# A routing table made one stage later, and the order of scatters around a stage boundary

## The reference

```python
h = _layernorm(x, axis=-1) * (1 + ca) + sa
x = x + ga * _L0_attn_ref(h, ...)            # projections, a scan over time, a GELU network
h = _layernorm(x, axis=-1) * (1 + cb) + sb
x = x + gb * _L0_ffn_ref(h, ...)

# _L0_ffn_ref
gate_scores = softmax(einsum('btd,ed->bte', x, Wg))
topk_val, topk_idx = top_k(gate_scores, 2)   # shares, normalised to sum 1
for e in range(8):
    a, b = split(x @ W1[e].T + b1[e])
    out += ((a * sigmoid(b)) @ Wo.T + bo) * comb[..., e:e + 1]
```

## Time and profile before

| what | value |
|---|---|
| median of 3 runs | 766.77 us (761.83 to 767.51) |
| the profiled execution | 773.54 us, its span 771.7 us |
| busy: PE, PE weight load, DVE | 661.6, 517.8, 628.0 us |
| busy: ACT, POOL | 476.1, 534.8 us |
| mean granted clock of TensorE | 0.926 of full speed |
| DMA | 93.50 MB in 104898 packets |

### The profile page before, as it was taken

One profiled execution on the slowest core, in us unless ns is written; L12 is line 12 of the kernel. 1 busy time (PEld: TensorE's weight loads), 2 busy tenths in 40 slices (PEclk: granted clock), 3 DMA queues, 4 the chain that ended last, 5 costly groups with the idle time before them and its releaser, 6 DMA issues. The chain is left out here.

```text
span 771.7 us, 14151 instructions
## 1 busy us (share of the span) xinstructions
PE 661.6 (86%) x3705; PEld 517.8 (67%) x3705; DVE 628.0 (81%) x1408; ACT 476.1 (62%) x1167; POOL 534.8 (69%) x623
## 2 busy tenths in 40 slices
PE   2666799999999798988888978248999999999995
PEld 0443577777777566776666767036888888888884
DVE  5399999999999999989999467734777777777774
ACT  3665778999998696877656667212444444444442
POOL 4476767988888777899778754763655655655656
PEclk8798999999999999999999888566999999999998
DMA  4998888999898777878887486752444334434420
GB/s 118 253 135 131 100 129 136 132 131 157 147 139 152 95 126 123 138 169 157 139 149 138 125 254 180 201 153 64 80 68 81 71 62 71 74 64 78 77 49 2
DMA packets 104898, 93.50 MB, mean 121 GB/s; under 512 B 16251, under 2 KB 84438, under 8 KB 104694
## 3 DMA queue, kind: packets, MB, share of 16 engines
q1 hardware_dynamic: 87446, 77.62, 55.4%
q0 software_dynamic: 16176, 12.75, 9.5%
q10 hardware_dynamic: 1200, 2.23, 0.9%
HBM read 34.03 MB, written 25.61 MB: 77 GB/s over the span
## 5 line engine op out<-in xcount | busy, mean ns | idle before, releaser
L1870 POOL DMA_INDIRECT out<-res,index x91 | 141.3, 1553 | 103.2 <-DVE res L1938 86.4
L773 POOL TENSOR_TENSOR rs_prod<-rT,state_rows 128x512 f32<-128x512 f32 x128 | 139.1, 1094 | 45.6 <-DVE state_rows L1395 43.8
L1390 DVE TENSOR_TENSOR kv<-key,v_spread 128x512 f32<-128x512 f32 x128 | 84.6, 670 | 7.9 <-DMA v_spread<-vT 6.4
L1843 ACT ACTIVATE sig<-ps_a 128x256 f32<-128x256 f32 x91 | 35.1, 386 | 87.1 <-PE ps_a L1782 66.0
L1395 DVE TENSOR_TENSOR_SCAN state_rows<-decay,state_rows,kv 128x512 f32<-128x512 f32 x64 | 79.9, 1269 | 0.2
L1395 DVE TENSOR_TENSOR_SCAN state_rows<-decay,kv 128x512 f32<-128x512 f32 x64 | 76.1, 1209 | 0.2
L1907 DVE SCALAR_TENSOR_TENSOR half<-ps_b,xg,sig 128x256 f32<-128x256 f32 x91 | 44.0, 484 | 39.1 <-ACT sig L1845 34.4
L1177 PEld LDWEIGHTS ps_k<-w,gel 128*128 128x128 f32 x512 | 61.5, 200 | 13.4 <-issue 11.1
L1845 ACT ACTIVATE sig<-ps_b 128x256 f32<-128x256 f32 x91 | 35.0, 385 | 54.9 <-PE ps_b L1782 48.2
L1900 DVE SCALAR_TENSOR_TENSOR ps_a<-ps_a,xg,sig 128x256 f32<-128x256 f32 x91 | 44.4, 487 | 27.8 <-ACT sig L1843 19.7
L1177 PE MATMUL ps_k<-w,gel 128*128 128x128 f32 x512 | 64.3, 286 | 1.2 <-ACT gel L1015 1.2
(11 more groups left out here) (316 smaller groups left out, 2016.4 us busy)
## 6 DMA issues: line engine op xcount, KB each, us to landing
v_spread<-vT SPq DMA_DIRECT2D x128, 256.0 KB, 5.2
xg<-sorted_scratch SPq DMA_DIRECT2D x91, 130.0 KB
xin<-in_L_attn_x SPq DMA_DIRECT2D x16, 256.0 KB, 6.5
x<-in_L_attn_x SPq DMA_DIRECT2D x16, 256.0 KB, 5.2
out<-x SPq DMA_DIRECT2D x16, 256.0 KB
sorted_scratch<-gel SPq DMA_DIRECT2D x4, 910.0 KB, 8.2
tokens_scratch<-h SPq DMA_DIRECT2D x12, 256.0 KB
stage<-tokens_scratch SPq DMA_DIRECT2D x16, 128.0 KB, 4.8
```

Of the source, the lines that this page charges most:

```text
L773: pool.tensor_tensor(rs_prod[:, p, idx % 4], rT[p][:], state[idx][:, p * NT:(p + 1) * NT], ALU.mult).then_inc(s["rs_ready"], 1)
L1390: dve.tensor_tensor(kv[idx % 2][:], key[:], v_spread[idx % SPREADS][:], ALU.mult).then_inc(s["kv_ready"], 1)
L1870: pool.indirect_dma_start(out_rows, bass.IndirectOffsetOnAxis(ap=index[k % RESULTS][:, i:i + 1], axis=0), res[k % RESULTS][:, i, :], None, ...
```

## The change

- The early table is made with the counts after twelve of batch 2's sixteen groups (`IN_FRONT` = 12), so it gives 16 groups instead of 20. Only these twelve groups are scattered in the first stage; batch 2's other four join batch 3's sixteen in `list_late`, and the second stage's waits count 12 and 20.
- The early table's two columns are turned by PE in the turn of the last logits (`turn_table`) and copied by DVE at the start of the next turn (`keep_table`).
- The late table's twenty steps are made by DVE in the second stage, ten after pair 0's joins and ten after pair 1's; PE turns them into free parts of `ps_y` in front of the projections of pairs 2 and 3, and DVE copies them in pairs 3 and 4. SP and PE wait for `tables_set` at group 16, DVE for `left_set` at the first late pair.
- Batch 1's pair 6 is listed at spot 15, ahead of the layer norm operations of the last tile, instead of at spot 18; pair 7 stays at spot 19.
- On SP the `h3` stores of tiles 13 to 15 move from their place to the end of the turn.

The core of the diff:

```diff
+IN_FRONT = 12
-        self.end = off[:, :, off.shape[2] - 1:off.shape[2]].rearrange("p e g -> p (e g)")
+        self.end = off[:, :, end:end + 1].rearrange("p e g -> p (e g)")
...
-    early_groups = (EARLY * NT - (CLASSES - 1) * P) // P // 2 * 2
+    early_groups = (EARLY * NQ - (RG - IN_FRONT) - (CLASSES - 1)) // 2 * 2
...
                 for t, p, b in tile(8):
-                    after(sp, s["h3_ready"], t)
-                    if not isinstance(t, int) or t < early:
-                        sp.dma_start(pay_tiles[t], h3[p][:]).then_inc(s["h3_stored"][p], 16)
-                    else:
...
+                    if not isinstance(t, int) or t < VECTOR_ROWS:
+                        store_rows(t, p)
...
                 for t, p, b in tile(2):
                     spread_value(0, t, p)
                     spread_value(1, t, p)
+                for t, p, b in tile(8):
+                    if isinstance(t, int) and t >= VECTOR_ROWS:
+                        store_rows(t, p)
...
-                if r == LISTED - 2 and spot % 2 == 1 and spot < RG - 2:
+                if r == LISTED - 2 and spot % 2 == 1 and spot <= RG - 1:
                     list_pair(r, spot // 2 - 1)
-                if r == LISTED - 2 and spot >= RG + 2:
-                    list_pair(r, spot - RG // 2 - 4)
+                if r == LISTED - 2 and spot == RG + 3:
+                    list_pair(r, RG // 2 - 1)
...
-                    for m in range(RG // 2):
+                    for m in range(IN_FRONT // 2):
                         list_pair(r, m)
...
+                    beside(t, LAST, turn_table)
...
+            def turn_table():
+
+                pe.wait_ge(s["small_ready"], 1)
+                pe.wait_ge(s["table_step"], Table.EARLY_STEPS)
+                for c in range(2):
+                    mm = pe.transpose(ps_k1[0:1, c * P:(c + 1) * P], at[:, c:c + 1], ident[:])
+                mm.then_inc(s["table_ps"], 1)
...
-            run_pipeline(step, {WEIGHTS_AT: prepare_weights, BIAS_AT: split_bias, TABLE_AT: early_table})
-            late_table()
-            dve.wait_ge(s["table_ps"], 1)
...
+            run_pipeline(step, {WEIGHTS_AT: prepare_weights, BIAS_AT: split_bias, TABLE_AT: early_table, TABLE_AT + 1: keep_table})
...
                 if j == early_groups:
 
-                    sp.wait_ge(s["listed"], 16 * RG)
+                    sp.wait_ge(s["tables_set"], 1)
+                    sp.wait_ge(s["listed"], 16 * (2 * RG - IN_FRONT))
...
+                if k == TABLE_AT:
+                    pe.wait_ge(s["table_step"], Table.LATE_STEPS)
+                    for i, c in enumerate((4, 3)):
+                        pe.transpose(ps_y[0:1, (2 + i) * P:(3 + i) * P], at[:, c:c + 1], ident[:])
+                if k == TABLE_AT + 1:
+                    pe.matmul(ps_y[:, 2 * P:3 * P], at[:, 5:6].broadcast_to([P, P]), ident[:], start=True, stop=True)
...
-                for n in range(RG):
-                    g = LATE_BATCH + n
+                for n in range(IN_FRONT, 2 * RG):
+                    g = LAST_BATCHES + n
...
+                if k == 0:
+                    table.late_sizes()
+                    table.late_gaps()
+                    table.before()
+                    table.weigh_pairs()
+                    table.pairs()
+                if k == 1:
+                    table.weigh_rows()
+                    table.rows()
+                    table.late_place()
+                    table.class_ends()
+                    table.step_back()
+                if k == TABLE_AT + 1:
+                    keep_table()
+                if k == TABLE_AT + 2:
+                    leave_out()
```

More of the change, by code:

```diff
@@ L188, with __init__ @@
     EARLY_STEPS, LATE_STEPS = 14, 20
-    def __init__(self, dve, stepped, count, off, starts, pair_steps, ones, column, column1, work, done, at, stride):
+    def __init__(self, dve, stepped, count, off, starts, pair_steps, ones, column, column1, work, done, at, stride, end):
         self.dve, self.stepped, self.count = dve, stepped, count
@@ L369, in attention_block @@
      work, done, at, hits, mask, sel, pos, tot, off, carry_on, small, share, rs_prod, bias_all, v_spread, early_groups, late_groups, early) = kept
-    left_out = work[:].rearrange("p a e -> p (a e)")[:, 0:late_groups]
     NH2 = out_w.shape[1]
@@ L662, in step, with store_rows @@
                     spread_value(1, t, p)
+                for t, p, b in tile(8):
+                    if isinstance(t, int) and t >= VECTOR_ROWS:
+                        store_rows(t, p)
+            def store_rows(t, p):
+                after(sp, s["h3_ready"], t)
+                if not isinstance(t, int) or t < early:
+                    sp.dma_start(pay_tiles[t], h3[p][:]).then_inc(s["h3_stored"][p], 16)
+                else:
+                    sp.wait_ge(s["rs_ready"], TILES * DK)
+                    sp.dma_start(last_rows[:, (t - early) * NQ + RG:(t - early + 1) * NQ + RG, 0:P], h3[p][:]).then_inc(s["h3_stored"][p], 16)
             def stage_pair(r, m):
@@ L1305, in _ @@
             run_pipeline(step, {FIRST_PRODUCT_AT: await_weights, GATE_AT: await_gate})
-            pe.wait_ge(s["logits_ready"], TILES)
-            pe.wait_ge(s["table_step"], Table.EARLY_STEPS + Table.LATE_STEPS)
-            for i, c in enumerate((0, 1, 4, 3)):
-                pe.transpose(ps_m[0:1, i * P:(i + 1) * P], at[:, c:c + 1], ident[:])
-            pe.matmul(ps_k1[:, 0:P], at[:, 5:6].broadcast_to([P, P]), ident[:], start=True, stop=True).then_inc(s["table_ps"], 1)
         @block.vector
@@ L1619, in early_table @@
                 dve.wait_ge(s["route_step"], LISTED * Router.STEPS)
-                table = Table(dve, s["table_step"], 0, off[:], starts[:], pair_steps[:], ones[:, 0:CLASSES], column[:, 0:1], column[:, 1:2], work[:], done[:], at[:, 0:2], STRIDE)
+                table = Table(dve, s["table_step"], 0, off[:], starts[:], pair_steps[:], ones[:, 0:CLASSES], column[:, 0:1], column[:, 1:2], work[:], done[:], at[:, 0:2], STRIDE, IN_FRONT)
                 table.early_sizes()
@@ L1628, in early_table, with keep_table @@
                 table.place()
-            def late_table():
-                dve.wait_ge(s["route_step"], BATCHES * Router.STEPS)
-                table = Table(dve, s["table_step"], Table.EARLY_STEPS, off[:], starts[:], pair_steps[:], ones[:, 0:CLASSES], column[:, 0:1], column[:, 1:2], work[:], done[:], at[:, 2:6], STRIDE)
-                table.late_sizes()
-                table.late_gaps()
-                table.before()
-                table.weigh_pairs()
-                table.pairs()
-                table.weigh_rows()
-                table.rows()
-                table.late_place()
-                table.class_ends()
-                table.step_back()
+            def keep_table():
+                dve.wait_ge(s["table_ps"], 1)
+                dve.tensor_copy(row_table[:, 0:early_groups], ps_k1[0:1, 0:early_groups])
+                dve.tensor_scalar(pair_table[:, 0:early_groups], ps_k1[0:1, P:P + early_groups], float(H2 * PACK), None, ALU.add)
             def add_last(t, p, b):
@@ L1698, in expert_block @@
     PAIRS, EARLY_PAIRS = (GROUPS + 1) // 2, early_groups // 2
-    LOADS, RESULTS = 6, 4
-    LATE_BATCH = early * NQ
+    LOADS, RESULTS, TABLE_AT = 6, 4, 2
+    LAST_BATCHES = early * NQ - RG
     with ExitStack() as ctx:
@@ L1751, in load_group @@
                 if j == 0:
[L1752 removed]
+                    sp.wait_ge(rows_listed, 16 * IN_FRONT)
                 sp.dma_start(xg[:, slot(j), :], sorted_dram[bass.ds(row, P), :]).then_inc(s["x_in"][k % LOADS], 16)
@@ L1935, in finish @@
                     late = 2 * k - early_groups
+                    if late == 0:
+                        dve.wait_ge(s["left_set"], 1)
                     dve.tensor_tensor(index[k % RESULTS][:, 0:n], number, left_out[:, late:late + n], ALU.add)
@@ L1942, in _, with keep_table, leave_out @@
             dve.tensor_copy(parts[:], parts_f[:]).then_inc(s["parts_set"], 1)
+            def keep_table():
+                dve.wait_ge(s["y_ps"], TABLE_AT + 1)
+                dve.tensor_copy(row_table[:, early_groups:], ps_y[0:1, 2 * P:2 * P + late_groups])
+                dve.tensor_scalar(pair_table[:, early_groups:], ps_y[0:1, 3 * P:3 * P + late_groups], float(H2 * PACK), None, ALU.add).then_inc(s["tables_set"], 1)
+            def leave_out():
+                dve.wait_ge(s["y_ps"], TABLE_AT + 2)
+                dve.tensor_scalar(left_out, ps_y[:, 2 * P:2 * P + late_groups], column[:, 0:1], float(TILES * NT), ALU.is_gt, ALU.mult).then_inc(s["left_set"], 1)
+            table = Table(dve, s["table_step"], 0, off[:], starts[:], pair_steps[:], ones[:, 0:CLASSES], column[:, 0:1], column[:, 1:2], work[:], done[:], at[:, 2:6], STRIDE, RG)
             for n in range(E // 2):
```

13 lines of the change are left out of this document (4 added, 9 removed).

## The result

| | before | after |
|---|---|---|
| median of 13 runs each, one chip | 765.8 us (761.8 to 767.5) | 761.1 us (758.9 to 763.5) |
| the profiled execution | 773.5 us | 761.1 us |
| ratio of the times | | 0.9947, 95% interval 0.9930 to 0.9964 |

The changed kernel is 4.7 us faster there, half a per cent. The number forecast was 761.3.

The account below looks back on a forecast made before the run. PE sets the expert stage's pace, 5.28 us a pair; at the seam all engines wait for the last. Terms -6.5 + 0.6 + 0.4 = -5.5 us, from the median 766.8 to 761.3; own range 758 to 764, widened to 756.5 to 768.

Parts of the forecast that it names:

- The seam: Between the two stages: DVE's first expert-stage operation comes 6.5 us earlier, bounds 5.1 to 7.2.
- The table and PE's turning of it: At the first stage's end: DVE's path loses twenty table steps, PE's turning and five operations, 6.85 us.
- The last power: Before the last logits: starts up to 0.9 us late behind the moved pair, 0.2 us of it on the path.
- Moving the stores in SP's queue: Late in the first stage: lets the moved pair's stage loads come up to 1.0 us earlier.
- POOL's own gain: At the seam: four scatters fewer and one pair moved ahead, so POOL arrives 7.1 to 7.6 us earlier.
- The early table's copies: Before DVE's last peak: PE's two transposes and DVE's copies put the peak 0.5 us later on the path.
- The expert stage: Added work in the second stage: PE's transposes and matmul 0.6 us, DVE's table steps 0.4 us.
- rival 2: Timed runs have no slow stretch; the seventh pair's load comes up to 1.6 us late; -3.3, 763.5 us; chance 0.15.
- The late listing: POOL at the expert stage's head: twenty scatters instead of sixteen take 26.1 us, ending at 524.1.
- The slow stretch: Unexplained delays behind the seam, some 10 us lost; forecast to keep its length and move with the seam, chance 0.42.
- rival 1: The slow stretch ends with the late scatters, only 1.5 us earlier; -1.5, 765.3 us; chance 0.25.
- Rival 4: Late scatters run 1.75 us apart and the slow stretch lasts until they end; 776.2 us; chance 0.08.

Follow-up runs that it names:

- g1: Kernel before, with a 128x512 memset on GpSimd behind each of its 16 late scatters to space them; 767.4 us, ratio 1.0028.
- e4: Kernel before, unchanged, run again on another chip for a second profile; 779.8 us, ratio 1.0003.
- e2: Changed kernel with SP's h3 stores of tiles 13 to 15 back in their old place; 776.0 us, ratio 0.9981 to the kernel before.
- e1: Changed kernel with batch 1's pair 6 listed behind the last power again; 777.2 us, ratio 0.9992 to the kernel before.
- f1: Changed kernel, unedited, on another chip; 775.8 us against 775.8 for the kernel before, ratio 0.9986.
- f3: Changed kernel with 16 late scatters at the expert stage's head, the last four behind the first two pairs' result scatters; 769.1 us, ratio 0.9910 to the kernel before.
- f4: Changed kernel with twelve late scatters at the head, eight behind the first four pairs' result scatters; 773.7 us, ratio 0.9977 to the kernel before.
- f5: f4 with e1's edit and ten of batch 2's scatters before the seam, so fourteen late ones at the head; 780.3 us, ratio 1.0065 to the kernel before.
- g2: Changed kernel with GpSimd waiting for the first two pairs' gates midway through its 20 late scatters; 766.6 us, ratio 1.0013 to the kernel before.
- g3: Changed kernel with a 128x256 memset on GpSimd behind each of its 20 late scatters; 765.0 us, ratio 0.9986 to the kernel before.
- g4: f3's kernel once more on another chip; 759.5 us, ratio 0.9915 to the kernel before.
- e3: Changed kernel with the late table made at the first stage's end again, twelve scatters in front and twenty behind; 781.8 us, ratio 1.0048 to the kernel before.

## Why the prediction was right, and where it was not

**The seam** (forecast 6.5 earlier, 5.1 at the least, at 497.0 to 498.2; measured 4.05, at 499.90). Taken apart, with both profiles: the last scan starts 1.0 later (424.7 to 425.7; this lies ahead of all that was changed), scan to power takes 51.4 in place of 49.2, power to peak 8.8 in place of 8.7, peak to DVE's end 11.5 in place of 18.4, and the hand-over behind it 2.45 in place of 2.89. That is 1.0 + 2.2 + 0.1 - 6.9 - 0.4 = -4.0. The first of these is chance, and so is part of the second: nine profiles with the pair moved have scan to power at 50.4 to 51.7, mean 51.1; five with it in its old place have 49.2 to 50.8, mean 50.1. Over several profiles the seam's gain is 7.0 from the peak on (14.0 in five of after's kind against 21.3 in before and 20.7 in g1; e4's 23.9 is left out) less 1.0 and 0.1, so **5.9**, close to the 6.5. It is a mean of unlike ones: before and g1 differ by 2.2 us from the scan to the seam (79.3 and 81.5). Term by term:

- *The table and PE's turning of it, 6.85*: right.
- *The last power, "up to 0.9 late, 0.2 on the path".* About 1.0 late, all of it on the path. I took the order of SP's queue as what held the moved pair's loads. The waits of SP in the changed kernel show another holder, the data of the pair of scatters before them (us in total, times, longest):

```profile
SPq L680 <- DMA sorted_scratch<-stage,dest: 4.7, 3, 2.1
```

  The loads go into buffers that are free only when an earlier pair's scatters have landed. They were there at 474.1, not 471.9. Moving the stores in SP's queue, which I gave 1.0 us, does nothing for that, as e2 shows. The move of the pair isn't waste all the same: without it (e1) POOL ends the seam 2.5 later behind the peak. Most of that comes back, since scan to power and power to peak are 0.7 shorter each: from the last scan to the seam e1 takes 75.3 us against e2's 74.2. POOL's own gain was forecast as 7.1 to 7.6 (its last front scatter ending at 494.61); it ended at 497.86 in place of 502.21, 4.35 earlier. The power began 3.2 us later, which took back what the moved pair gave: the first front scatter starts at 481.96, where it was at 481.92.
- *The early table's copies, 0.5 on the path.* DVE waited 1.81 us for PE before them (485.76), more than the 1 us allowed, but for most of that it would have waited for ACT's logits. These were there at 485.52:

```profile
485.32 0.20 ACT L973 ACTIVATE logits<-ps_m 128x32 f32<-128x32 f32 x1 [0.99 <-PE ps_m L1226]
```

  PE had turned the table by 485.72, and the peak began at 485.93, 0.4 us behind the logits; in the kernel before it followed them by 0.03 (482.62, 482.65). So the forecast size was about right and ACT's copy was no cover. It hardly shows in the time from power to peak (8.8 in place of 8.7), because ACT's logits came 0.3 us sooner behind the power.

**The expert stage** (forecast +1.0). This is the term of the sum that failed. g1's first five intervals are those of the kernel before with no stretch: 5.47, 4.11, 5.36, 5.26, 5.26. The changed kernel's ten are 5.47, 4.39, 5.88, 5.65, 5.47, 6.06, 5.67, 5.26, 5.26, 5.28. Against g1, and 5.26 from the sixth on, it loses 0.3 in the second, 0.5 and 0.4 where DVE's two lots of steps stand, 0.2 for PE's transposes of the table, and 1.2 at the seventh pair's load, together **2.6**. DVE's two lots cost 0.9 where I had put 0.4, PE's transposes 0.2 where I had put 0.6 for all of PE's work, and for the 0.3 I have no cause; the load is what I put at nothing in the forecast and left to rival 2. With the stretch it isn't seen (f1's sixth and seventh intervals are 5.48 and 5.27). The steps in the trace, the first and last of either ten:

```profile
513.89 0.19 DVE L211 SCALAR_TENSOR_TENSOR work<-off,starts 128x28 f32<-128x28 f32 x1
...
516.00 0.18 DVE L225 TENSOR_REDUCE at<-work 128x1 f32<-128x28 f32 x1
...
518.86 0.18 DVE L228 TENSOR_TENSOR work<-work 128x28 f32<-128x28 f32 x1
...
520.75 0.16 DVE L273 TENSOR_TENSOR at<-at 128x1 f32<-128x1 f32 x1
```

**The late listing** (forecast 26.1 us, measured 25.84, from 500.47 to 526.31). The scatters are 1.26 us apart but for the first two (1.29 and 1.50 long), beside DVE's wide subtractions from 500.25 on. In f1, beside the same subtractions, the second took 0.96. The steps of the table beside the others cost them nothing, as the trace before had it. The Trainium skill's page "SBUF — State Buffer", section "Who interferes with whom", which I had weighed against that row, is borne out beside the subtractions, which read two wide SBUF inputs, and in front of the seam beside the router's scan over 128x476 (a scatter at 494.06 took 1.26), but not beside the table's small steps.

**The slow stretch.** The forecast (0.42) said that it keeps its length and moves with the seam. No run shows that. Where it comes up, in nine profiles, it ends with the run of late scatters, which is rival 1 (0.25). I had priced that rival at -1.5, and by the losses it is -5.9 + (15.7 - 9.9) = -0.1: f1's medians give 0.0. Where it doesn't come up, rival 2 (0.15) holds, at -5.9 + 2.6 = -3.3. That this is to the tenth what I had given it is luck: I had it from -6.5 and +3.2.

With these terms the runs can be told together. For each, the seam's gain (5.9; 4.5 in e1, 6.9 in f5, 0 in g1) and the loss of its profile against the kernel before's with the stretch (9.9) on A and B, without it (-0.8) on C and on the first chip:

| kernel | sum | measured (difference of medians) |
|---|---|---|
| f1 (B) | -5.9 + 5.7 = -0.2 | 0.0 |
| f3 (B) | -5.9 + 0.9 = -5.0 | -6.8 |
| f4 (B) | -5.9 + 5.0 = -0.9 | -2.2 |
| f5 (B) | -6.9 + 10.1 = +3.2 | +4.5 |
| e1, e2 (A) | -4.5 + 5.4 = +0.9, -5.9 + 5.8 = -0.1 | -1.6, -2.8 |
| g1 (C) | 0 + 3.7 = +3.7 | +2.3 |
| g2 (C) | -5.9 + 9.0 = +3.1 | +1.5 |
| g3 (C) | -5.9 + 8.2 = +2.3 | 0.0 |
| g4 (C) | -5.9 + 2.1 = -3.8 | -5.6 |
| after (first chip) | -5.9 + 2.6 = -3.3 | -4.7 |

(e3 is left out, and f3 and f4 have the common 5.9, since their profiles lost time in front of the seam as well.) The order within each set is right; the sizes are not explained to better than 2 or 3 us.

On A the only profile of the kernel before, e4's, lost 7.4 us in front of the seam, which the table leaves out. The four profiled executions with such a loss (e3, e4, f3, f4) took 3.6 to 6.8 us more than their kernels' medians, the other four on A and B within 1.3 of theirs, so the usual execution has less of it or none. Were 2.6 us of it usual in the kernel before on A, e1 and e2 would fit. No run shows that.

On C and on the first chip all five lie 1.4 to 2.3 below their sums. On C part of this may be the 5.9: by C's own profiles the time from the last scan to the seam is 81.5 us in g1 and 73.2 to 74.5 in g2, g3 and g4, a gain of 7.5, and with it g2, g3 and g4 come to 1.5, 0.7 and -5.4. On the first chip 1.4 us stay open. A stretch of 10 us in a few executions of the kernel before doesn't account for them: its profiled execution took 773.5 us, but none of its 13 timed ones took more than 767.5, 1.7 above their median. So it is unlikely that the executions timed there had the stretch that the profile shows and the forecast was reckoned from.

So the prediction's -5.5 came out at -4.7 in part by luck. The seam's gain was nearly as forecast, the stage term was 1.6 too small, which gives -3.3, and what made up the rest isn't known. It was right in its number and, over several profiles, in the seam; the account of the stretch, on which its chance rested, was wrong.

**What would show it.** 5.28 a pair unchanged: right. Last late scatter at 523.5 to 525: 526.31, by the later seam. Fourth pair's transposes at 527.7 (forecast) or 531 to 533 (rival 1): 520.09 without the stretch, 536.92 in f1 with it. DVE's wait for the early table under 1 us: 1.81, of which 0.4 on the path. Rival 4's 1.75 us a scatter came up in no run. By its own signs the prediction was wrong in two places: POOL came to the seam after DVE (497.86 and 497.46), and the slow stretch behaved otherwise.

## What to carry to other kernels

Work moved out of a hand-over buys what it occupied there, but the queue that pays for it (here four scatters more on GpSimd behind the hand-over) must be followed to the consumer that waits for its end, and at the queue's own pace, not at that of the bounding engine. Four entries left out of the run and put between later ones were worth more on chip B (6.8 us) than the whole change gained on any chip (4.7). And where a trace shows a delay that no dependency explains, take several profiles on several chips before building a sum on it.

## What the runs showed of the hardware that I had not expected

While GpSimd issues indirect scatters one behind the other (0.96 us each, 0.30 between), SP's instructions can fall to about one in 0.70 us, and PE, ACT and DVE begin some of theirs microseconds late, while others on DVE keep their pace. It begins some 6 to 11 us behind the first scatter of the run (nine profiles), on SP in f4 later still, and SP's last slow instruction lies between 2 us before and 2.5 behind the end of the run. SP's register moves, 29 ns by median, take up to 722, and ACT begins operations 5 us after their inputs are there. It isn't bound to the start of a stage. In f3's profile the same loss stands in front of the seam, beside the twelve scatters of batch 2 from 478.5 to 493.6: PE starts its selection matmul after 6.98 us of "issue" where f1 has 4.82 for DVE, and the peak comes 13.6 us behind the power in place of 8.8. The profiles of e3, e4 and f4 have it there too (11.1, 13.6 and 12.2 from power to peak).

```profile
492.34 1.83 PE L1239 MATMUL ps_m<-sel,ones 128*128 128x448 f32 x2 [6.98 <-issue]
```

```profile
491.75 1.83 PE L1238 MATMUL ps_m<-sel,ones 128*128 128x448 f32 x2 [4.82 <-DVE small L127]
```

It depends on the chip or on the execution: all eight profiles on A and B have it, none of four on C, and on the first chip one of two. What in the chip is held up isn't settled. The DMA engines aren't full, busy for 39% of the time from 505 to 537 in f1 (the last but one number):

```profile
505.00:537.00 32.00, 18.85 (x59) 14.57 (x60) 11.40 (x40) 5.95 (x14) 16.82 (x18) 0.66 0.39 124
```

Whether spacing or a pause in the run avoids it stays open, since the chip that ran those kernels never showed it.
